# Three small VectorE steps in two-tensor forms, and the first raw multi-head scores ahead of the last multi-head values

## What is computed

```python
xn = layernorm(x)
# branch 1: latent attention, 16 heads, content part 16 and rotary part 64 wide, causal
q, k = concat(q_c, rope(q_r)), concat(k_c, rope(k_r))
s = softmax(mask(q @ k.T * SCALE)) @ v @ w_out.T
# branch 2: multi-head attention (16 heads of 16, causal), then a mixture of experts
xr = xn + softmax(mask(q2 @ k2.T * scale)) @ v2 @ Wo.T        # of rmsnorm(xn)
y  = rmsnorm(xr)
top_logits, top_idx = top_k(y @ Wr.T, 2)                      # 8 experts, 2 for each token
probs = softmax(top_logits)                                   # the gates
g = silu(xr + sum over the two experts e of probs[e] * Wd[e] (silu(Wg[e] y) * (Wu[e] y)))
return x + s * g
```

## Time and profile before

| | |
|---|---|
| median of 3 runs | 810.94 us (809.0 to 813.9) |
| profiled execution, its own time | 808.98 us |
| its span, first to last instruction | 807.2 us |
| PE busy | 726.7 us, 90% |
| DVE busy | 551.0 us, 68% |
| ACT busy | 429.0 us, 53% |
| POOL busy | 387.9 us, 48% |
| mean granted clock of PE | 0.953 |

### The profile page before, as it was taken

The page is one execution under the profiler, slowest core; times in us unless marked ns, Lnnn a source line. Parts: engine busy times, 40 slices in busy tenths (PEclk is TensorE's granted clock), DMA queues, the critical chain, the costliest instruction groups (busy, mean ns, idle before and its releaser), DMA issues.

```text
span 807.2 us, 17047 instructions
## 1 busy us (share of the span) xinstructions
PE 726.7 (90%) x5968; PEld 651.0 (81%) x5968; DVE 551.0 (68%) x1925; ACT 429.0 (53%) x895; POOL 387.9 (48%) x489
## 2 busy tenths in 40 slices
PE   4869999999999999999999999894799999999970
PEld 3858978978988987887888887572699999999970
DVE  3876567687587586586586596425488888888844
ACT  2434364365365365355355445451487777887752
POOL 3642452354453453463563464253455666556640
PEclk9978999999999999999999999777799999999995
DMA  9492663573473474384284186431889999999736
GB/s 293 109 177 48 92 152 74 78 163 77 64 159 83 64 151 103 50 161 107 40 159 107 43 159 160 140 104 30 234 204 240 230 230 229 262 275 254 170 36 217
DMA packets 81416, 115.54 MB, mean 143 GB/s; under 512 B 17475, under 2 KB 57667, under 8 KB 81283
## 3 DMA queue, kind: packets, MB, share of 16 engines
q1 hardware_dynamic: 70612, 101.74, 53.0%
q0 software_dynamic: 9856, 12.13, 8.5%
q10 hardware_dynamic: 864, 0.60, 0.3%
HBM read 70.06 MB, written 23.46 MB: 116 GB/s over the span
## 4 chain that ended last, share of the span: by engine, by line
PE 69%; DVE 12%; DMA 6%; issue 4%; ACT 4%; SPq 4%; POOL 2%; DVEq 0%; POOLq 0%; ACTq 0%
PE ps L703 63%; DVE ex L1572 2%; ACT ex L1299 2%; DVE stg L1571 2%; DVE ps L1631 2%; DMA qt<-stg 2%; PE ps L739 2%; SPq L446 2%; PE ps L1097 1%; DVE ps L1628 1%; DMA ln<-in_w_ln 1%; POOL stg L607 1%; PE ps L748 1%; SPq L458 1%; SPq L402 1%
## 5 line engine op out<-in xcount | busy, mean ns | idle before, releaser
L647 POOL TENSOR_SCALAR_AFFINE_SELECT ex<-ex 128x256 f32<-128x256 f32 x256 | 102.9, 407 | 169.8 <-ACT ex L1299 157.7
L1299 ACT ACTIVATE ex<-ps 128x384 f32<-128x384 f32 x240 | 115.8, 490 | 122.3 <-PE ps L703 118.5
L703 PE MATMUL ps<-qt,kt 81*128 81x128 f32 (+2 forms) x768 | 165.5, 330 | 4.2 <-issue 2.0
L1628 DVE CUSTOM_DVE_ANT_0 ps<-ps,mask 128x128 f32<-128x128 f32 x256 | 78.1, 305 | 74.3 <-PE ps L703 72.6
L703 PEld LDWEIGHTS ps<-qt,kt 81*128 81x128 f32 (+1 forms) x768 | 111.1, 197 | 15.8 <-issue 7.9
L607 POOL TENSOR_TENSOR stg<-stg,ex 128x512 f32<-128x512 f32 x64 | 82.5, 1291 | 80.2 <-DVE ex L1572 78.3
L1631 DVE CUSTOM_DVE_ANT_0 ps<-ps,mask 128x256 f32<-128x256 f32 x256 | 119.1, 465 | 0.0
L690 POOL DMA_INDIRECT expert_rows<-yo,slot_of x46 | 75.4, 1639 | 82.6 <-ACT yo L1419 63.1
L1456 DVE TENSOR_TENSOR wel<-raw,weh 128x768 fp32r<-128x768 f32 x92 | 87.7, 956 | 18.3 <-ACT weh L1150 18.3
L703 PE MATMUL ps<-xth,wh 128*128 128x256 f32 x384 | 78.9, 286 | 2.0 <-issue 2.0
L1571 DVE TENSOR_TENSOR stg<-ps,cos_t 128x512 f32<-128x512 f32 x64 | 44.1, 689 | 52.8 <-PE ps L703 45.8
(11 more groups left out here) (157 smaller groups left out, 1682.1 us busy)
## 6 DMA issues: line engine op xcount, KB each, us to landing
raw<-in_w_experts SPq DMA_DIRECT2D x92, 384.0 KB, 4.5
qt<-stg SPq DMA_DIRECT2D x64, 128.0 KB, 4.0
kt<-stg SPq DMA_DIRECT2D x64, 128.0 KB, 3.8
multi_heads<-stg SPq DMA_DIRECT2D x64, 128.0 KB, 2.4
qt<-multi_heads SPq DMA_DIRECT2D x32, 192.0 KB, 3.6
kt<-multi_heads SPq DMA_DIRECT2D x32, 128.0 KB, 3.4
qt<-stg SPq DMA_DIRECT2D x8, 256.0 KB, 4.6
kt<-stg SPq DMA_DIRECT2D x8, 256.0 KB, 6.1
```

What stands on the lines that cost most here:

```text
L647: nc.gpsimd.affine_select(a, a, [[0, 2], [1, P]], ALU.is_ge, zero, 0, -1).then_inc(exm, 1)
L703: return nc.tensor.matmul(o, a, m, start=start, stop=stop, skip_group_check=True, **k)
L1299: nc.scalar.activation(ex[:, h % (2 * G), :], ps[4 + h % 2][:, P:4 * P], ACT.Exp, scale=scale).then_inc(ex_, 1)
L1628: nc.vector.tensor_tensor_reduce(out=o[:, 0:P], in0=o[:, 0:P], in1=mask2[:, 1, :], scale=-1.0, scalar=-2.0 * BIG, op0=ALU.add, op1=ALU.min ...
```

## The change

Two things are changed. On DVE, `stepped` and `plus_one` are now a `scalar_tensor_tensor` that takes the same tensor as both inputs (add the constant, then the maximum with the tensor itself, which is the sum), and the copy in `both` is now a `tensor_tensor` maximum of `gsum` with itself. On PE, `stage_t2` no longer calls its last values; it returns them through `batch`, and the next batch calls them behind its two raw multi-head scores. The sets of heads that stand ahead are written as tuples, which changes no order.

```diff
--- before.py
+++ after.py
@@ -880,8 +880,8 @@
                     if h >= 2:
                         wait(pe, ex_, 16 * b + h - 1)
                     scores_t(h, ps[4 + h % 2]).then_inc(st, 1)
-                    if h in ahead:
-                        max_head(ahead[h])
+                    for n in ahead.get(h, ()):
+                        max_head(n)
                     if h == H - 2:
                         tail()
                     if h >= G and h % G == G - 1:
@@ -906,7 +906,7 @@
                     pe.wait_ge(s_one, 16)
                     wait(pe, v1d, b + 1)
                 return heads(b, scores1, st1, ex1, exm1, pv1, ov1, v1, before_h0, lambda: wait(pe, x2d, b), max2(b),
-                             {h: h + 2 for h in range(H - 2)}, lambda: None, after)
+                             {h: (h + 2,) for h in range(H - 2)}, lambda: None, after)
 
             def last_t2(after):
                 def before_h0():
@@ -948,9 +948,9 @@
                     if h == 1:
                         wait(pe, roped, 8 * (b + 1) + 8)
                     return scores2(h, o)
-                ahead = {h: h + EARLY for h in range(8)} | {h: h + 3 for h in range(9, 13)}
-                heads(b, scores, st2, ex2, exm2, pv2, ov2, v2, before_h0, lambda: wait(pe, sd, b + 1), max_head, ahead,
-                      lambda: max_t1(b + 1), after)()
+                ahead = {h: (h + EARLY,) for h in range(8)} | {h: (h + 3,) for h in range(9, 13)}
+                return heads(b, scores, st2, ex2, exm2, pv2, ov2, v2, before_h0, lambda: wait(pe, sd, b + 1), max_head,
+                             ahead, lambda: max_t1(b + 1), after)
 
 
             def route_transpose(r):
@@ -986,7 +986,7 @@
 
                 stage_p1(b, after | {"mk": lambda: (head(0), head(1)), "q3": lambda: head(2), "k3": lambda: head(3)})
 
-            def batch(b, first, more):
+            def batch(b, first, more, values_before):
                 to_tokens = None
                 after1 = {}
                 if not first:
@@ -997,6 +997,7 @@
                     max2(b)(0)
                     max2(b)(1)
                     if not first:
+                        values_before()
                         to_tokens()
                     after1[10] = lambda: transpose_x(b + 1)
                     last_values = stage_t1(b, after1)
@@ -1012,10 +1013,11 @@
                         if not first:
                             route_ranks(b - 1)
                     p1_with_m1(b + 1, {"nq": after_first, "k0": between, "k1": back})
-                    stage_t2(b, max1(b + 1), {2: project, 5: lambda: project_v2(b + 1)})
+                    return stage_t2(b, max1(b + 1), {2: project, 5: lambda: project_v2(b + 1)})
                 else:
                     max2(b)(0)
                     max2(b)(1)
+                    values_before()
                     to_tokens()
                     for h in range(H):
                         if h % 2 == 0:
@@ -1079,11 +1081,11 @@
             project_v2(0)
             pe.wait_ge(cast, 1)
             pe.wait_ge(s_c, 16 * 4)
-            batch(0, True, True)
+            values_left = batch(0, True, True, None)
             pe.wait_ge(wrd, 1)
             for b in range(1, last):
-                batch(b, False, True)
-            batch(last, False, False)
+                values_left = batch(b, False, True, values_left)
+            batch(last, False, False, values_left)
 
 
             def rows_transpose(blk):
@@ -1744,7 +1746,8 @@
                 def stepped():
                     dve.wait_ge(pst, 6 * r + 6)
                     step = rc[:, C_IDS:C_IDS + 8].rearrange("p (a f) -> p a f", f=2)
-                    nc.vector.tensor_scalar(step[:, :, :], step[:, :, :], 2.0 * P, None, ALU.add).then_inc(gst, 1)
+                    nc.vector.scalar_tensor_tensor(out=step[:, :, :], in0=step[:, :, :], scalar=2.0 * P, in1=step[:, :, :],
+                                                   op0=ALU.add, op1=ALU.max).then_inc(gst, 1)
                 return in_expert, chosen, summed, kept, stepped
 
             def gate_steps(r):
@@ -1752,7 +1755,8 @@
 
                 def plus_one():
                     dve.wait_ge(gex, r + 1)
-                    nc.vector.tensor_scalar(gsum[:, :], gexp[:, :], 1.0, None, ALU.add).then_inc(gst, 1)
+                    nc.vector.scalar_tensor_tensor(out=gsum[:, :], in0=gexp[:, :], scalar=1.0, in1=gexp[:, :],
+                                                   op0=ALU.add, op1=ALU.max).then_inc(gst, 1)
 
                 def inverse():
                     dve.wait_ge(gst, 3 * r + 2)
@@ -1760,7 +1764,7 @@
 
                 def both():
                     dve.wait_ge(gst, 3 * r + 3)
-                    copy(g[:, :, 0], gsum[:, :])
+                    nc.vector.tensor_tensor(g[:, :, 0], gsum[:, :], gsum[:, :], ALU.max)
                     nc.vector.tensor_tensor(g[:, :, 1], gexp[:, :], gsum[:, :], ALU.mult).then_inc(posd, 1)
                 return plus_one, inverse, both
```

## The result

| | before | changed |
|---|---|---|
| median of 12 runs | 811.33 us (806.87 to 826.68) | 813.52 us (812.14 to 816.38) |
| profiled execution, its own time | 808.98 us | 812.22 us |
| its span | 807.2 us | 810.5 us |

The ratio is 1.0039, with a 95% interval from 1.0021 to 1.0058: 3.2 us slower, at most 4.7 and at least 1.7. The forecast was 812.9 us, +2.9. The time and the place are as predicted, one term of the sum was too small, and the trace of this one execution holds two large differences that are not the change's.

A forecast was written before the change was run, and what follows sets the result against it. PE was taken to bound the kernel (69% of the chain). Forms 0, seams +2.2 and landings +0.7 make +2.9 us on a base of 809.97: 812.9 us, range 808.2 to 816.5.

The forecast's parts named there:

- The forms: DVE's small steps in the projection stage: the new two-tensor forms stay held until POOL ends, 0 us won or lost.
- two rows beside POOL's selects: Trace rows at 525.06 and 544.92 us: small two-input DVE forms took 0.35 and 0.29 us, ending with POOL.
- The row that spoke the other way: Large SCALAR_TENSOR_TENSOR on DVE, 28.17 to 30.11 us, ran through a POOL TENSOR_TENSOR without being held.
- The first rival: DVE's two forms run free beside POOL's sums in the projection stage: 1.5 us won, 811.4 us; chance 0.18.
- The seams: PE behind batches 0 to 6: transposes wait for ACT's copy, +0.31 us at each of seven seams, 2.2 us.
- The landings: Raw scores moved ahead at the seams wait for loaded multi-head rows: +0.7 us over seven, ends 0 and 4.0.
- 4.7 us seam: Seam after the loads issued from 241.64 us: slowest landing took 4.7 us, so raw scores could wait 0.57 us.
- the landing of the batch at 425.8 us: Second landing example: it took 4.2 us, where up to 4.1 needs no wait, so 0.1 us of waiting.
- The base: Starting time for the whole kernel, 809.97 us: the middle of the profiled time and three runs, before adding the sum.
- The second rival: Raw scores wait for their rows' landing at every seam: 6.2 us, giving 816.1 us; chance 0.13.
- The third: At all seven seams ACT does not hold the transposes and the 0.28 us wait goes: -2.0 us, 808.0; chance 0.09.
- DVE wins nothing from earlier maxima: Latent half after the seam: first two maxima come about 1.1 us earlier, but nothing there waits for DVE; 0 won.

The follow-up runs named there:

- forms_only: The kernel before with only the three DVE steps in their new two-tensor forms, nothing moved; ratio 1.0002 (0.9977 to 1.0026).
- the probe: Separate kernel computing nothing of the block: ten small DVE operations, each beside a POOL sum; old and new forms held alike, the first new one ending at 14.86, POOL at 14.84.
- steps_gone: The kernel before without the step of `rc` and the copy into `meta`, at the same result; ratio 1.0021 (0.9991 to 1.0052).
- tokens_early: The changed kernel with three of the eight transposes allowed to start before ACT's last copy; ratio 1.0018 (0.9997 to 1.0039).
- one_ahead: The changed kernel with only head 0's raw scores ahead of the last values, head 1's behind them; ratio 1.0036 (1.0016 to 1.0056).

## Why the prediction was right, and where it was not

- **The forms, 0 us: right.** 1.15 and 1.28 us, ending with POOL's sum, and forms_only at 1.0002. The choice rested on two rows beside POOL's selects; the probe shows the same beside its sums. The row that spoke the other way (28.17 us) was set aside because DVE had begun first there; no run tested that order. The first rival (0.18) was wrong.
- **The size of that rival: about right, for a reason only half seen.** It said that DVE, once free, would wait for the DMA of its seventh product and win 0.13 us a batch. steps_gone, with half the hold gone, won 0.20, and the DMA wait grew from 1.5 to 8.4 us. That PE's clock could fall was not in the prediction at all.
- **The seams, 7 x 0.31: right.** 2.80 to 2.81 instead of 2.50 us wherever no row was late, to the hundredth; the wait for ACT is 0.5 us by the profile, 0.57 from start to start. That filling it takes the price away is shown by the traces of tokens_early and one_ahead; their timings (1.0018 and 1.0036) do not set them apart from the changed kernel.
- **The landings, +0.7 us: too small.** They were 1.7 us in the trace of the changed kernel, 1.2 in the mean of thirteen. The reading of the earlier trace rows was right for its own trace, where the excess sums to 0.6 us; the step that failed is taking that one trace for all. The late landing of the 4.7 us seam comes back in every trace, by 0.5 us in the mean; those of the seams at 370 and 308 us, which the prediction did not look at, come in eleven and nine; the landing of the batch at 425.8 us, which was taken as the second example, is hardly ever late. Four seams waited, by up to 0.80 us, where one to three by at most 0.6 were foretold, and a batch became 0.56 us longer from seam to seam (62.89 instead of 62.33), not 0.3 to 0.4. With 1.2 the sum would have been +3.4 us; measured is +3.2 (1.7 to 4.7), which cannot tell +2.9 from +3.4.
- **The base, 809.97 us: a little low, and partly luck.** The median before was 811.33 over twelve runs, that of the changed kernel 813.52. That this is within 0.6 us of the forecast says less than the ratio does.
- **The second rival, landing waits at all seams (816.1): wrong.** Three of seven waited not at all.
- **The third, that the move earns its wait: wrong.** No seam had the transposes behind the last values at once.
- **DVE wins nothing from earlier maxima: right.** PE's wait for the maxima stood at 5.9 us before and 6.8 after.

## What to carry to other kernels

Before a piece of work is moved into a wait, look at what it hides where it stands: here the raw scores stood in the shadow of a copy that was exactly as long as they, and moving them into one wait of 0.28 us opened another of 0.57. A small operation held by another engine is not cured by another form with the same ports; it needs a form with one SBUF input that is no copy and no tensor_scalar, an input in PSUM, or another moment, and the operation behind it must be looked at too, since it may be held in its place. A wait that is removed on the feeding engine can come back in TensorE at another place, so the granted clock of the stretch behind it has to be read as well as the waits.

## What was not expected of the hardware

- A reciprocal of SBUF data is not held by GpSimd's sum (0.17 us with and without), while a copy of two elements is (0.88).
- TensorE's granted clock fell to half for most of 4 us in 8 of 34 projection stages in which it waited 0.58 us for a product of DVE shortly ahead of the output projection, and in none of 54 in which it waited earlier, for 1.1 to 1.3 us at once or for two waits of 0.3 to 0.8. Each fall cost 1.7 us.
- In the last batch the part of the time at half clock differed between two executions of the same kernel: a mean of 0.66 and 0.72 over the same 30 us, 0.83 in the changed kernel. The time from the last seam's transposes to those of the last batch went with it: 39.7 and 37.9 us, and 36.1 in the changed kernel. Differences of 2 us between single traces of one kernel can come from there.
